# Dense blocks over 512 consecutive nodes in a graph-convolution kernel: 60 edge tiles per block in place of 56

## What is computed

```python
def gcn_conv(x, src, dst, w, W, b, n):          # called twice, with W1 and W2
    xw = x @ W
    deg = segment_sum(w, dst, n)
    dinv = where(deg > 0, rsqrt(deg), 0.0)
    norm = dinv[src] * w * dinv[dst]
    return segment_sum(xw[src] * norm[:, None], dst, n) + b

x = x + relu(batchnorm(gcn_conv(relu(gcn_conv(layernorm(x), ...)), ...)) + layernorm(x))
x = x + top2_mixture_of_8_experts(layernorm(x))
```

## Time and profile before

| | us |
|---|---|
| median of 3 runs (lowest, highest) | 2394.96 (2393.16, 2397.04) |
| profiled execution | 2393.27 |
| its span, first to last instruction | 2391.5 |
| PE busy | 1907.5 (80%) |
| POOL busy | 1667.1 (70%) |
| DVE busy | 951.1 (40%) |
| ACT busy | 425.3 (18%) |

### The profile page before, as it was taken

The page is one execution under the profiler, slowest core; times in us unless marked ns, Lnnn a source line. Parts: engine busy times, 40 slices in busy tenths (PEclk is TensorE's granted clock), DMA queues, the critical chain, the costliest instruction groups (busy, mean ns, idle before and its releaser), DMA issues.

```text
span 2391.5 us, 29967 instructions
## 1 busy us (share of the span) xinstructions
PE 1907.5 (80%) x8514; PEld 1349.8 (56%) x8515; DVE 951.1 (40%) x2679; ACT 425.3 (18%) x1140; POOL 1667.1 (70%) x1678
## 2 busy tenths in 40 slices
PE   1044529999999988859989999999864638999997
PEld 0044315555555556645556565565543527999997
DVE  7999211222222234522223233242338772333332
ACT  0900100000000001100000000000015563444443
POOL 0877777777777777757777777777748345666675
PEclk9999769999999999979999999999975558999999
DMA  9992615556565645545555565565661136888885
GB/s 311 340 313 77 195 41 178 192 190 204 185 201 193 191 150 151 151 128 174 175 180 192 175 197 176 182 195 176 192 217 63 60 131 161 209 213 206 212 213 124
DMA packets 264137, 431.16 MB, mean 180 GB/s; under 512 B 39408, under 2 KB 147631, under 8 KB 263887
## 3 DMA queue, kind: packets, MB, share of 16 engines
q1 hardware_dynamic: 181199, 253.79, 31.9%
q0 software_dynamic: 81088, 173.80, 27.7%
q10 hardware_dynamic: 1728, 2.13, 0.3%
HBM read 339.36 MB, written 91.16 MB: 180 GB/s over the span
## 4 chain that ended last, share of the span: by engine, by line
POOL 57%; issue 20%; DMA 9%; PE 7%; DVE 6%; ACT 1%; POOLq 0%; SPq 0%; DVEq 0%; ACTq 0%
POOL arena L581 44%; POOL pair_weights L566 9%; DMA out_dram<-ACC 7%; PE psum L1695 3%; PE psum L1703 2%; POOL out_dram L656 1%; DVE edge_cols L1227 1%; DVE stats L1233 1%; DVE X L1230 1%; DMA rows_for_experts<-ACC 1%; PE psum L1644 0%; DVE ACC L1336 0%; POOL ACC L644 0%; DVE ACC L1222 0%; PE psum L1686 0%
## 5 line engine op out<-in xcount | busy, mean ns | idle before, releaser
L581 POOL DMA_INDIRECT arena<-conv_rows,edge_cols x1120 | 1065.8, 952 | 354.9 <-issue 340.9
L1521 PE MATMUL psum<-arena,X 128*128 128x512 f32 x1568 | 747.4, 601 | 39.0 <-DMA arena<-pair_weights 25.9
L1569 PE MATMUL psum<-arena 128*128 128x256 f32 x2240 | 598.9, 394 | 141.9 <-DMA arena<-conv_rows,edge_cols 131.3
L1569 PEld LDWEIGHTS psum<-arena 128*128 128x128 f32 x2240 | 422.1, 196 | 369.1 <-issue 270.5
L1521 PEld LDWEIGHTS psum<-arena,X 128*128 128x128 f32 x1568 | 300.6, 193 | 258.1 <-issue 212.6
L1157 DVE TENSOR_TENSOR ACC<-ACC,psum 128x256 f32 x80 | 33.8, 422 | 916.7 <-PE psum L1539 916.3
L566 POOL DMA_INDIRECT pair_weights<-scale_b,mean_b x224 | 225.5, 1007 | 121.8 <-issue 68.0
L1133 DVE TENSOR_SCALAR arena<-iota,edge_cols 128x128 f32<-128x128 f32 x1120 | 296.7, 365 | 3.5 <-issue 3.4
L656 POOL DMA_INDIRECT out_dram<-ACC x105 | 166.2, 1583 | 109.4 <-DMA out_dram<-ACC 83.7
L1695 PE MATMUL psum<-ACC,arena 128*128 128x128 f32 x1680 | 207.6, 277 | 0.2 <-DVE ACC L1369 0.2
L735 ACT ACTIVATE arena<-psum 128x256 f32<-128x256 f32 x80 | 30.5, 381 | 984.6 <-PE psum L1569 984.6
(11 more groups left out here) (291 smaller groups left out, 1408.1 us busy)
## 6 DMA issues: line engine op xcount, KB each, us to landing
arena<-pair_weights SPq DMA_DIRECT2D x371, 256.0 KB, 4.7
arena<-in_L_ffn_W_dram SPq DMA_DIRECT2D x113, 512.0 KB, 8.0
pair_weights<-zeros SPq DMA_DIRECT2D x4, 12544.0 KB, 46.7
arena<-conv_rows,edge_cols POOLq DMA_INDIRECT x1120, 2.8
conv_rows<-X SPq DMA_DIRECT2D x13, 896.0 KB, 4.9
X<-in_x_dram SPq DMA_DIRECT2D x12, 896.0 KB, 11.3
rows_for_experts<-ACC SPq DMA_DIRECT2D x7, 910.0 KB, 4.3
arena<-pair_weights SPq DMA_DIRECT2D x3, 1792.0 KB, 17.7
```

The source lines that it names most:

```text
L581: pool.indirect_dma_start(G[:, n * D:(n + 1) * D], None, y_tab[layer], bass.IndirectOffsetOnAxis(srcT[:, t:t + 1], 0)).then_inc(gathered[n ...
L1521: ins = m.matmul(bank(6 + c, BW), X[:, t * D + c * P:t * D + (c + 1) * P], table, start=(t == 0), stop=(t == NT - 1))
L1569: ins = m.matmul(bank(2 * (k % 2), D), S[:, n * P:(n + 1) * P], G[:, n * D:(n + 1) * D], start=(j == 0), stop=(j == GT - 1))
```

## The change

There are now 17 dense groups (`DG`), 238 tiles, and 39 gathered ones. The four blocks no longer consist of whole groups: they hold 60, 60, 60 and 58 tiles (`STEP`, `BLOCKS`). A block's 512 columns are 512 consecutive nodes from the destination of its first edge (`block_f`, `block_i`) rather than four spans of 128. Tables and units keep their size and number. The cell number takes the position in the block (`in_block`), and the test of the data gets the condition that this lies between 0 and 511. DVE adds a finished block with one instruction. PE's signals that a slot is free come also after every third unit of a group. `EARLY` takes over the 21 of `BEFORE`, and the loop between the two has no iterations. `blocks_under` is rewritten for the new bounds.

```diff
 GT = 14
 OH = 8
 WIN = 448
-DG = 16
-BG = 4
+DG = 17
+NB = 4
+STEP = 60
+BW = 512
...
-    BW = BG * P
     CELLS = NB * NP * BW
     UNITS = NB * NT
     PACE = GT * P * N // E
     GG = NG - DG
+    BLOCKS = [(b * STEP, (b + 1) * STEP if b < NB - 1 else DT) for b in range(NB)]
...
+        in_block = early(DT)
...
+        block_f, block_i = sb("block_f", NB), sb("block_i", NB, I32)
...
         def blocks_under(t):
             
 
-            g = next(g for g in range(NG + 1) if finished(g) > t)
-            under = [d for d in range(min(g, DG)) if PACE * d + SLACK + P > P * t]
-            return under[-1] // BG + 1 if under else 0
+            starts = [lo // GT for lo, _ in BLOCKS]
+            under = [b for b, g in enumerate(starts)
+                     if PACE * g - SLACK < P * (t + 1) and PACE * (g + 1) + SLACK + BW > P * t]
+            return under[-1] + 1 if under else 0
...
                     if b == 1:
                         load_x()
-                    sp.dma_start(pairs[b * NP * BW:(b + 1) * NP * BW, :].rearrange("(p r c) o -> p r (c o)", p=P, c=D),
-                                 zeros[:, :].unsqueeze(1).broadcast_to([P, NP * BW // (P * D), D])).then_inc(filled[b], 16)
+                    sp.dma_start(pairs[b * NP * BW:(b + 1) * NP * BW, :].rearrange("(p r c) o -> p r (c o)", p=P, c=BW // 2),
+                                 zeros[:, 0:BW // 2].unsqueeze(1).broadcast_to([P, NP * 2 // P, BW // 2])).then_inc(filled[b], 16)
...
-                            sp.wait_ge(paired[n // NT], 16 * BG * GT)
-                        sp.dma_start(early_at[q].rearrange("p (u c) -> p u c", c=BW),
+                            sp.wait_ge(paired[n // NT], 16 * (BLOCKS[n // NT][1] - BLOCKS[n // NT][0]))
...
-                g.iota(cell_at.rearrange("p (b k t) -> p b k t", b=NB, t=GT), [[NP * BW // P, NB], [1, BG], [0, GT]], base=0,
-                       channel_multiplier=0, allow_small_or_imprecise_dtypes=True)
+                for b, (lo, hi) in enumerate(BLOCKS):
+                    g.memset(cell_at[:, lo:hi], float(b * NP * BW))
...
-                            for r in range(b * BG * GT // 2, (b + 1) * BG * GT // 2):
+                            for r in range(BLOCKS[b][0] // 2, BLOCKS[b][1] // 2):
...
+                chain(v.tensor_scalar(block_f[:, :], bank(6, NG + NB)[:, NG:NG + NB], float(NP - BW), None, ALU.min))
+                v.tensor_copy(block_i[:, :], block_f[:, :])
+                even = (NB - 1) * STEP
+                v.tensor_tensor(in_block[:, 0:even].rearrange("p (b t) -> p b t", t=STEP),
+                                dstT[:, 0:even].rearrange("p (b t) -> p b t", t=STEP),
+                                block_f[:, 0:NB - 1].unsqueeze(2).broadcast_to([P, NB - 1, STEP]), ALU.subtract)
+                chain(v.tensor_tensor(in_block[:, even:DT], dstT[:, even:DT],
+                                      block_f[:, NB - 1:NB].broadcast_to([P, DT - even]), ALU.subtract))
...
+                v.tensor_reduce(bad[:, 1:2], in_block, AX_X, ALU.max)
+                chain(v.tensor_reduce(bad[:, 0:1], in_block, AX_X, ALU.min))
+                chain(v.tensor_scalar(bad[:, 3:4], bad[:, 1:2], float(BW - 1), bad[:, 3:4], ALU.is_gt, ALU.add))
+                chain(v.tensor_scalar(bad[:, 3:4], bad[:, 0:1], 0.0, bad[:, 3:4], ALU.is_lt, ALU.add))
...
-                                                 in1=by_half(dst_rel[:, 0:DT], h), op0=ALU.mult, op1=ALU.add))
-                    chain(v.scalar_tensor_tensor(out=cell[:, cells], in0=by_half(cell_at, h), scalar=float(P),
-                                                 in1=cell[:, cells], op0=ALU.mult, op1=ALU.add))
+                                                 in1=by_half(in_block, h), op0=ALU.mult, op1=ALU.add))
+                    chain(v.tensor_tensor(cell[:, cells], by_half(cell_at, h), cell[:, cells], ALU.add))
...
                         def add_block(b):
-                            for k in range(BG):
-                                n = DG * layer + b * BG + k
-                                at = base_of(b * BG + k)
-                                if k == 0:
-                                    dve.wait_ge(dense_used, UNITS * layer + (b + 1) * NT)
-                                dve.wait_ge(added, GG * layer + so_far[0])
-                                dve.wait_ge(dense_added, n)
-                                a = acc[:, :, bass.ds(at, P)]
-                                v.tensor_tensor(a, a, psum[:, 6:8, k * P:(k + 1) * P], ALU.add).then_inc(dense_added, 1)
-                            so_far[1] += BG
+                            at = dve.value_load(block_i[0:1, b:b + 1], min_val=0, max_val=NP - BW)
+                            dve.wait_ge(dense_used, UNITS * layer + (b + 1) * NT)
+                            dve.wait_ge(added, GG * layer + so_far[0])
+                            dve.wait_ge(dense_added, NB * layer + b)
+                            a = acc[:, :, bass.ds(at, BW)]
+                            v.tensor_tensor(a, a, psum[:, 6:8, 0:BW], ALU.add).then_inc(dense_added, 1)
+                            so_far[1] += 1
...
+                m.matmul(bank(6, NG + NB)[:, NG:NG + NB], ones[0:1, :], dstT[0:1, 0:NB * STEP:STEP], start=True,
+                         stop=True).then_inc(base_bc, 1)
...
+                        for n in range((EARLY, 0)[layer], BEFORE[layer]):
+                            dense(n, 1)
...
-                                    pe.wait_ge(gathered[n // 2], 32 * (GG // 2 * layer + k // 2 + 1))
+                                    pe.wait_ge(gathered[n // 2], 32 * (len(range(k % 2, GG, 2)) * layer + k // 2 + 1))
...
-                                    tells = d == units - 1 or n_unit % NT == NT - 1
+                                    tells = d == units - 1 or d % 3 == 2 or n_unit % NT == NT - 1
```

More of the change, by code:

```diff
@@ L87, in gnn_ffn @@
     GG = NG - DG
-    assert NG % (2 * DQ) == 0 and DQ * GT * P <= 2 * GT * D + 2 * GT * P + ASLOTS * BG * P
+    assert NG % (2 * DQ) == 0 and DQ * GT * P <= 2 * GT * D + 2 * GT * P + ASLOTS * BW
     RH = HALO + RW + HALO
@@ L91, in gnn_ffn @@
     assert HW == P
-    assert NB * BG == DG and DR * RW == DT * P and DR <= P and UNITS % ASLOTS == 0 and GG % 2 == 0
+    BLOCKS = [(b * STEP, (b + 1) * STEP if b < NB - 1 else DT) for b in range(NB)]
+    assert all(lo < hi and lo % 2 == 0 for lo, hi in BLOCKS) and NB * STEP <= EC
+    assert DR * RW == DT * P and DR <= P and UNITS % ASLOTS == 0
     assert CELLS + DT * P < 2 ** 24 and MAXIN % 8 == 0 and MAXIN < HALO
@@ L293, in gnn_ffn @@
         ROW_LOADS = 8
-        BEFORE = (21, 0)
-        assert BEFORE[0] % ASLOTS == 0 and NT % ASLOTS == 0 and (UNITS - BEFORE[0]) % ASLOTS == 0
+        BEFORE, EARLY = (21, 0), 21
+        assert EARLY <= BEFORE[0] and NT % ASLOTS == 0 and (UNITS - EARLY) % ASLOTS == 0
         SETS = -(-NT // 4)
@@ L451, in load_pairs @@
                 def load_pairs(layer):
-                    for n in range(BEFORE[layer], UNITS):
+                    for n in range((EARLY, 0)[layer], UNITS):
                         m = layer * UNITS + n
@@ L1154, in add_group @@
                             dve.wait_ge(added, GG * layer + k)
-                            dve.wait_ge(dense_added, DG * layer + so_far[1])
+                            dve.wait_ge(dense_added, NB * layer + so_far[1])
                             a = acc[:, :, bass.ds(at, P)]
@@ L1411, in _ @@
                 pe.wait_ge(dstT_set, 1)
-                m.matmul(bank(6, NG), ones[0:1, :], dstT[0:1, 0:ET:GT], start=True, stop=True).then_inc(base_bc, 1)
+                m.matmul(bank(6, NG), ones[0:1, :], dstT[0:1, 0:ET:GT], start=True, stop=True)
+                m.matmul(bank(6, NG + NB)[:, NG:NG + NB], ones[0:1, :], dstT[0:1, 0:NB * STEP:STEP], start=True,
+                         stop=True).then_inc(base_bc, 1)
                 turn_edges(1, w_row)
@@ L1518, in unit @@
                             if t == 0 and b + NB * layer:
-                                pe.wait_ge(dense_added, BG * (NB * layer + b))
+                                pe.wait_ge(dense_added, NB * layer + b)
                             for c in range(KC):
@@ L1525, in dense @@
                         def dense(n, used):
-                            mm = layer * UNITS + n - BEFORE[0]
+                            mm = layer * UNITS + n - EARLY
                             u = mm % ASLOTS
@@ L1545, in aggregate @@
                                 turn_set(n)
-                            sets, batches = 3, BEFORE[0] // ASLOTS
+                            sets, batches = 3, EARLY // ASLOTS
                             for q in range(batches):
@@ L1585, in aggregate @@
                                     blocks = NB if layer == 0 else blocks_under(FINISH[1][0][i])
-                                    if DG * layer + blocks:
-                                        pe.wait_ge(dense_added, DG * layer + BG * blocks)
+                                    if NB * layer + blocks:
```

(3 more changed lines are left out.)

12 lines of the change are left out of this document (6 added, 6 removed).

## The result

The kernel after takes 2379.84 us (median of 4 runs, 2377.75 to 2382.35), the one before, run beside it, 2394.06 (4 runs, 2393.00 to 2397.04). The ratio is 0.9939, interval 0.9922 to 0.9956: 14.2 us faster between the medians, where 11.8 had been forecast. The forecast time of 2383.2 is 3.4 us too high, inside the range. The profiled execution took 2381.91 us with a span of 2380.1, 11.4 less than the span before; forecast were 2381.5 and 2379.7.

A forecast was written before the change was run, and what follows sets the result against it. POOL's count of indirect DMAs times their pitch was taken to bound the kernel until 1772 us. Terms -35.2 + 17.7 + 2.1 + 3.6 = -11.8 us gave 2383.2 us from the median, range 2378 to 2391.

The forecast's parts named there:

- rival A: Inside the layers: PE, not POOL, sets their end, so the change costs +8.4 us, time 2403.4; chance 0.07.
- Scatters, +17.7: Before the first gather: fourteen more scatters of pair weights on POOL, 1.263 us each, all on the path, 17.7 us.
- rival C: No measurable difference: stretched scatters, 10.5 us in all, double in number, leaving -1.3 us, time 2393.7; chance 0.08.
- Gathers, -35.2: In both layers: one group of 14 gathers fewer on POOL, 17.6 us saved per layer, 35.2 together.
- DVE at the start, +2.1: Before the first scatter: added DVE instructions delay POOL by 2.1 us, ends 1.3 and 2.3.
- The tail, +3.6: After layer 1's last sum: six linears left instead of three, three more at 1.20 us, 3.6 us longer.
- The boundary, 0: Between the layers: POOL's wait of 14.0 us stays as it was.
- the 15 us that I had named as a sign of error: Between the layers: more than 15 us there would show the forecast wrong.
- PE, adds, signals: 0: Inside the layers: PE's 7.5 us less work per layer, the single add and earlier signals change no time.
- The load of x, 0: Near the last gather: x moves 17.6 us closer, could delay landing by 4.0 us, costed at 0 as already drained.
- rival B: Layer 1's end: last gather lands 4.0 us late, tail slow, scatters at their mean: -5.7 us, time 2389.3; chance 0.16.
- The corners themselves: POOL's timeline: first scatter near 60.3 us, first gather 371.8, first of layer 1 1070.6, last 1756.0.

The follow-up runs named there:

- 56 tiles: Kernel after taken back to 56 dense tiles per block and 40 gathered groups, new code kept: 2394.13 us, ratio 1.0005 to the kernel before.
- six more products: Kernel after with six added products of identity by zeros on PE per gathered group: 2460.89 us, ratio 1.0280 to the kernel before.
- light PE: Kernel after with the upper 128 features left out of the dense products, save in each block's first and last unit: 2381.37 us, ratio 0.9956 to before.
- signals of before: Kernel after without the added signals that a slot is free inside a group: 2379.05 us, ratio 0.9940 to the kernel before.
- no test: Kernel after without the two reductions and two comparisons that test the block span: 2378.76 us, ratio 0.9942 to the kernel before.
- after again: Kernel after run a second time, unchanged: 2384.08 us, ratio 0.9939 to the kernel before.
- 11 in 2: Kernel after with 11 dense units per two groups in layer 1 instead of 16 per three: 2375.92 us, ratio 0.9929 to the kernel before.
- filled first end with 11 in 2: Kernel after with 11 dense units per two groups in layer 1 and products by zeros in layer 0's last two groups: 2373.83 us, ratio 0.9919 to before.
- filled ends: Kernel after with 18 products of identity by zeros in each of the last two groups of both layers: 2383.71 us, ratio 0.9944 to before.
- filled ends and 11 in 2: Kernel after with products by zeros in both layers' last two groups and 11 dense units per two groups in layer 1: 2382.10 us, ratio 0.9930 to before.
- three products more: Kernel after with three added products of identity by zeros on PE per gathered group: 2382.00 us, ratio 0.9954 to the kernel before.

## Why the prediction was right

*What bounds the kernel.* Right. Counts of indirect DMAs times their pitch gave the long stretches before, after, with 56 tiles and with fourteen scatters fewer, and 101 us less of PE's work in layer 0 (111 in layer 1) changed nothing. One step of the reasoning on rival A fails: the prediction held the rise of PE's period per group against the 7 us of room. With six more products the busy time rose by only 2.0 us per group, and the layers became 36 and 43 us longer, because lateness adds up from group to group.

*Scatters, +17.7.* Measured +17.74, and 17.5 when fourteen are taken away. The stretched ones early on did not multiply: in both traces they are eight, two of 1.3 us and six of 2.3 to 2.8 us, the latter beside the same instructions of DVE, and the mean stayed at 1004 ns (1007 before). So rival C had no mechanism.

*Gathers, -35.2.* Measured -37.5. 14 of the pitch of before are 17.6 per layer; the other 0.8 and 1.5 us are the pitch itself, 1.2532 in place of 1.2547 us in layer 0 and 1.2550 in place of 1.2578 in layer 1. Whether the change or the execution does that is open: in the second run of the kernel after it was 1.258 in layer 1.

*DVE at the start, +2.1.* Measured +2.58. The timeline of DVE shows the first of the added instructions in a row (L882 to L888) and the last (L913 to L916):

```profile
17.48 0.16 DVE L882 TENSOR_SCALAR block_f<-psum 128x4 f32<-128x4 f32 x1
17.68 0.17 DVE L883 CAST block_i<-block_f 128x4 int32<-128x4 f32 x1
17.75 0.34 DVE L885 TENSOR_TENSOR ACC<-edge_cols,block_f 128x180 f32<-128x180 f32 x1
18.01 0.21 DVE L888 TENSOR_TENSOR ACC<-edge_cols,block_f 128x58 f32<-128x58 f32 x1
18.26 0.97 DVE L890 TENSOR_TENSOR edge_cols<-edge_cols,base_f 128x784 f32<-128x784 f32 x1
...
23.88 0.40 DVE L913 TENSOR_REDUCE bad<-ACC 128x1 f32<-128x238 f32 x1
24.20 0.39 DVE L914 TENSOR_REDUCE bad<-ACC 128x1 f32<-128x238 f32 x1
24.63 0.21 DVE L915 TENSOR_SCALAR bad<-bad 128x1 f32<-128x1 f32 x1
24.88 0.21 DVE L916 TENSOR_SCALAR bad<-bad 128x1 f32<-128x1 f32 x1
25.12 0.52 DVE L917 TENSOR_REDUCE bad<-arena 119x1 f32<-119x352 f32 x1
```

18.26 - 17.48 = 0.78 and 25.12 - 23.88 = 1.24 us: 2.02, against 2.1. The other half microsecond is not these, and lies inside the spread of the twelve traces named above. Two terms of the forecast's sum are a little off, 0.21 for the 58 columns, where its own rule gives 0.16, and 0.15 for the cast, measured 0.17; both are too small to matter.

*The tail, +3.6.* Measured +3.25 in this trace, and the linears themselves as forecast. DVE's timeline, against the earlier trace rows:

```profile
1765.42 0.48 DVE L1093 SCALAR_TENSOR_TENSOR ACC<-psum,dinv,mean_b 128x256 f32<-128x256 f32 x1 [2.04 <-PE psum L1495]
...
1766.97 0.48 DVE L1093 SCALAR_TENSOR_TENSOR ACC<-psum,dinv,mean_b 128x256 f32<-128x256 f32 x1 [0.27 <-PE psum L1495]
...
1768.17 0.47 DVE L1093 SCALAR_TENSOR_TENSOR ACC<-psum,dinv,mean_b 128x256 f32<-128x256 f32 x1
...
1769.35 0.47 DVE L1093 SCALAR_TENSOR_TENSOR ACC<-psum,dinv,mean_b 128x256 f32<-128x256 f32 x1
...
1770.54 0.47 DVE L1093 SCALAR_TENSOR_TENSOR ACC<-psum,dinv,mean_b 128x256 f32<-128x256 f32 x1
...
1771.73 0.48 DVE L1093 SCALAR_TENSOR_TENSOR ACC<-psum,dinv,mean_b 128x256 f32<-128x256 f32 x1
```

Intervals of 1.55, 1.20, 1.18, 1.19 and 1.19: 6.31 us where three took 2.90, so +3.41, which is 1.14 per linear. The stretch before them is 0.83 us shorter and the one behind them 0.67 longer. The fast ones no longer wait for PE at all: it is DVE's three instructions per linear (0.48, 0.42 and 0.42 us) that make the 1.19. The Trainium skill (TensorE: Matmul & The Clock Gate, "Part 1: The HAM clock gate (the "warmup" mystery)") would have allowed the slow pace for all six, 5 x 1.70 = 8.5 us. The trace agrees with its other half, that activity releases the throttle: only the first interval is long, and the granted clock was 0.67 from 1764 to 1768 us and 0.96 from 1768 to 1774.

```profile
1764.00:1768.00 4.00, 4.00 (x14) 3.25 (x13) 2.24 (x6) 0.83 (x2) 0.00 (x0) 0.67 0.79 234
1768.00:1774.00 6.00, 2.92 (x12) 1.58 (x10) 5.29 (x14) 3.01 (x7) 0.00 (x0) 0.96 1.04 340
```

That the whole stretch came so near to the forecast is in part luck. The forecast priced the linears and put the clock's effect on the rest of the stretch at nothing. Over the 12 us from the last gather on, the granted clock was 0.51 before and 0.86 in this trace, and 1.00 in the second run of the kernel after:

```profile
1771.40:1783.40 12.00, 8.66 (x20) 5.78 (x21) 1.80 (x6) 0.80 (x2) 0.94 (x1) 0.51 0.36 94
1760.20:1772.20 12.00, 9.58 (x38) 6.48 (x38) 5.53 (x15) 2.05 (x5) 0.95 (x1) 1.00 0.45 112
```

In five traces with six linears (fourteen scatters fewer, light PE, signals of before, no test, after again) it was 1.00 and the stretch took 27.7 to 28.3 us, not 29.6. In the four with three linears and no filling at that end (before, 56 tiles, 11 in 2, filled first end with 11 in 2) it was 0.51 to 0.73 and the stretch took 26.4 to 27.7. So DVE does take some 1.2 us for each added linear, but with six of them left PE was also at a higher clock in this stretch (that the schedule does this was not tested by itself), and the stretch as a whole took 28.3 us in the mean of the six traces, this one counted, against 27.0 of the four: +1.3, not +3.6.

*The boundary, 0.* Mis-sized: +1.80, past the 15 us that I had named as a sign of error. What moved is PE's clock on the way over, not the change's work: the wait is 12.8 to 12.9 us in the four traces where the clock there stayed up (three and six products more, filled ends, filled first end) and 15.5 to 17.0 in the others, save 14.4 in the kernel with filled ends and 11 in 2, and 14.0 before. The granted clock over that stretch goes with them: 0.94 to 1.00 for the four, 0.88 for the 14.4, 0.83 for before's 14.0, 0.59 to 0.71 for all the rest. That the clock sets the wait is shown by the two kernels with filling there in which it stayed up. Why it was lower than in before is open: with 56 tiles the wait was 16.3 and with the signals of before 17.0, so neither the 60 tiles nor the signals are needed for it, and against before's one trace chance is not excluded.

*PE, adds, signals: 0.* Right. The eight adds take 1.22 us each, as forecast, and PE's wait for them fell from 13.1 to 5.2:

```profile
PE psum L1536 <- DMA arena<-pair_weights: 26.3, 1, 26.3
...
PE psum L1536 <- DVE ACC L1161: 5.2, 6, 3.3
```

*The load of x, 0.* Right in size, wrong in its reason, that x should have drained by then. In the last 13 us before the last gather the DMA engines' busy share was 0.99, where it had been 0.36 in the kernel before:

```profile
1758.40:1771.40 13.00, 8.23 (x30) 5.42 (x30) 2.91 (x7) 1.20 (x3) 9.67 (x11) 0.93 0.36 104
1743.00:1756.00 13.00, 8.79 (x32) 6.41 (x30) 2.68 (x7) 1.00 (x3) 9.69 (x11) 0.87 0.99 318
```

The last six gathers landed after 4.5 us in the median, against 3.0 before, the last two after 4.1 against 3.8, and PE began on the last pair 4.6 us after issue, against 4.3. So rival B's late landing was there, but only some 0.3 us of its 4.0 reached the end. More of it came in the kernel with three products more: share 1.08 between 1745 and 1758 us, the last two landed after 6.0, and the last pair was used 6.2 us after issue. With 11 in 2 the load of x starts 13 us earlier, the share is 0.35, and the last six landed after 3.1.

*The corners themselves.* The last gather came at 1756.04, to 0.1 us as forecast. That is luck: +0.5 at the start and +1.8 at the boundary were met by 2.3 us that the gathers saved beyond the forecast.

*What stays open.* The corners sum to -11.4 and the medians differ by 14.2. The profiled execution of the kernel after lies 2.1 us above its median, that of before 0.8 under its own; together these are the 2.8. The interval of the ratio spans -10.5 to -18.7 us, so no cause is needed, and none is shown. Part of it may be the tail, which in this execution was 1.3 to 1.9 us longer than in the five traces named there. Another place where executions differ by that much is the last stage, whose code nothing touches: it was between 589 and 594.5 us long in the fourteen traces.

## What to carry to other kernels

Where one engine issues short, equal instructions back to back with no wait but issue, count them: removed and added ones times their pitch gave every stretch here within 1.5 us. An engine at 93% need not be the next bound, but here its idle time was about all that could be added to it: 32 us more per layer were free, 79 us were not, with 48 idle. The smallest gap between its product and the one who waits for it (10.2 us here) says how late it may once come, not how much work it can take on. Filler work that keeps a clock up pays only where the engine then waits for something; put where it is already behind, it gives the gain back.

## What the runs showed of the hardware

An indirect DMA of 128 rows or words occupies POOL for 0.95 us (gathers) or 0.96 us (the last 32 scatters before the gathers) and is followed by 0.30, with PE 76 to 98% busy beside it. Six scatters at 97 to 113 us in the trace of before took 2.3 to 2.8 us; why was not tested. PE's granted clock at a boundary of some 15 us depends on what PE did just before: it was 0.71 over 12 us of it in the kernel after, 0.67 over 14 us in its second run, and 1.00 with filled ends, where POOL's wait was 2.9 and 2.6 us shorter; with the same filling and 11 in 2 it was 0.88. More work on PE made one stretch shorter, by keeping the clock at 1.00.
